# A graph attention, linear attention and mixture-of-experts layer: the waits of the first pass over the edges are given constants

## The reference

```python
xn = layernorm(x)                                   # x: 3125 nodes x 256
x = x + gnn(xn, edges) + mix(xn)                    # 53125 edges, sorted by dst, own edges included
x = x + ffn(layernorm(x))

def gnn(x, src, dst):                               # 4 heads of 64
    h = x @ W
    logits = leaky_relu(a_src(h)[src] + a_dst(h)[dst], 0.2)
    alpha = exp(logits - segment_max) / segment_sum(exp(...))
    return relu(segment_sum(alpha * h[src]) + bias)

def mix(x):                                         # 4 heads of 32
    q, k, v = x @ W_qkv; context = softmax(k over nodes)^T v
    return (q @ context) @ W_out + b_out

def ffn(x):                                         # 8 experts, 2 for each node, weighted
    return sum over the chosen e of w_e * (gelu(x @ W1[e] + b1[e]) @ W2[e] + b2[e])
```

## Time and profile before

| | us |
|---|---|
| three runs | 1038.55, 1036.66, 1035.8 |
| median | 1036.66 |
| span of the profiled execution | 1154.8 |
| the profiled execution's own time | none is recorded beside its span |

### The profile page before, as it was taken

The page is one execution under the profiler, slowest core; times in us unless marked ns, Lnnn a source line. Parts: engine busy times, 40 slices in busy tenths (PEclk is TensorE's granted clock), DMA queues, the critical chain, the costliest instruction groups (busy, mean ns, idle before and its releaser), DMA issues. The chain is left out here.

```text
span 1154.8 us, 18630 instructions
## 1 busy us (share of the span) xinstructions
PE 937.2 (81%) x5127; PEld 831.2 (72%) x5128; DVE 492.8 (43%) x1359; ACT 397.2 (34%) x1099; POOL 558.7 (48%) x572
## 2 busy tenths in 40 slices
PE   7949688676876678697577476699999999999995
PEld 6848577565666567576466364699999999999994
DVE  6664465565656456456457367511111111111110
ACT  4526242224324233233233222443333333333331
POOL 2254666666666666566656620523333333333331
PEclk8976867777678677667758676799999999999998
DMA  7333444444444434444434424865666555656561
GB/s 215 101 106 91 113 117 114 114 134 127 115 115 128 136 105 133 119 122 138 129 109 108 129 66 142 290 202 180 180 180 182 168 170 172 180 179 179 180 182 19
DMA packets 76492, 163.65 MB, mean 142 GB/s; under 512 B 11536, under 2 KB 40868, under 8 KB 76306
## 3 DMA queue, kind: packets, MB, share of 16 engines
q0 software_dynamic: 30144, 69.30, 24.6%
q1 hardware_dynamic: 45729, 93.15, 24.4%
q10 hardware_dynamic: 560, 0.52, 0.2%
HBM read 145.95 MB, written 16.99 MB: 141 GB/s over the span
## 5 line engine op out<-in xcount | busy, mean ns | idle before, releaser
L571 POOL DMA_INDIRECT gathered<-h_table,src_row x416 | 402.2, 967 | 227.1 <-issue 121.5
L890 PE MATMUL bank<-gathered,one_hot 128*128 128x260 f32 x832 | 289.8, 503 | 57.7 <-issue 39.0
L890 PEld LDWEIGHTS bank<-gathered,one_hot 128*128 128x128 f32 x832 | 202.9, 253 | 111.5 <-issue 73.7
L1714 ACT ACTIVATE hiddenT<-bank,b_slot 128x128 f32<-128x128 f32 x424 | 121.1, 369 | 248.7 <-PE bank L1747 248.7
L1692 POOL DMA_INDIRECT out<-y,add_index x53 | 84.4, 1593 | 246.3 <-DVE y L1805 122.9
L1747 PEld LDWEIGHTS bank<-xgT,acc 128*128 128x128 f32 x1696 | 200.0, 194 | 3.5 <-ACT xgT L1706 0.9
L1747 PE MATMUL bank<-xgT,acc 128*128 128x128 f32 x1696 | 200.4, 277 | 0.5 <-ACT xgT L1706 0.5
L834 PEld LDWEIGHTS bank<-adc,w_sb 128*128 128x128 f32 x832 | 141.6, 234 | 78.4 <-issue 67.9
L1769 PE MATMUL bank<-w_sb,hiddenT 128*128 x848 | 193.5, 381 | 0.0
L834 PE MATMUL bank<-adc,w_sb 128*128 x832 | 126.1, 269 | 74.0 <-issue 73.8
L1769 PEld LDWEIGHTS bank<-w_sb,hiddenT 128*128 128x128 f32 x848 | 157.0, 190 | 22.0 <-issue 1.9
(11 more groups left out here) (240 smaller groups left out, 670.9 us busy)
## 6 DMA issues: line engine op xcount, KB each, us to landing
acc<-in_L_ffn_W SPq DMA_DIRECT2D x53, 1024.0 KB
w_sb<-key_table SPq DMA_DIRECT2D x52, 256.0 KB
w_sb<-in_L_ffn_W SPq DMA_DIRECT2D x8, 1024.0 KB, 11.1
gathered<-h_table,src_row POOLq DMA_INDIRECT x416
h_table<-acc SPq DMA_DIRECT2D x25, 130.0 KB, 2.0
out<-w_sb SPq DMA_DIRECT2D x5, 512.0 KB
xn_table<-w_sb SPq DMA_DIRECT2D x5, 512.0 KB
xs<-in_x SPq DMA_DIRECT2D x3, 640.0 KB, 10.5
```

The lines of the kernel that those rows point to most:

```text
L571: pool.indirect_dma_start(gathered[:, r, j, :], None, h_table, bass.IndirectOffsetOnAxis(ap=src_row[:, t:t + 1], axis=0)).then_inc(gather_ ...
L890: mm = pe.matmul(sum_bank[r % SUMS][:, 0:ROW], one_hot[:, r, j, :], gathered[:, r, j, :], start=(j == 0), stop=(j == G - 1))
L1714: op = act.activation(hiddenT[:, k, g * P:(g + 1) * P], bank[1 + 2 * k + half][:, f * P:(f + 1) * P], ACT.Gelu, bias=b1_slot[:, k, g:g + 1])
```

## The change

The body of each engine's loop becomes a function `one_pass(c)`. The loop stays, and holds an If: where the pass counter isn't zero, the body is emitted as before with the register c; its Else holds the body emitted with c = 0, a Python integer, so that every count in it is a constant. The separate increments of `waited` inside the pass stay in the first and go from the second. DVE's two inner Ifs go: what they held stands in the plain body alone. The instructions of the pass are in the program twice, the general body first.

```diff
+            def every_pass(eng, passes, one_pass):
+                with eng.Fori(0, passes) as c:
+                    with eng.If(c != 0):
+                        one_pass(c)
+                    with eng.Else():
+                        one_pass(0)
+
+            def counted_wait(eng, c):
+                if not isinstance(c, int):
+                    eng.sem_inc(waited, 1)
...
                         sp.wait_ge(x_step, c * len(PIECES) + k + 1 + (k >= INSIDE))
-                        sp.sem_inc(waited, 1)
+                        counted_wait(sp, c)
...
-                    with sp.Fori(0, passes) as c:
+                    def one_pass(c):
                         sp.wait_ge(keys_ready, c + 1)
-                        sp.sem_inc(waited, 1)
+                        counted_wait(sp, c)
...
+                    every_pass(sp, passes, one_pass)
...
-                    with pool.Fori(0, passes) as c:
+                    def one_pass(c):
                         for s in range(NGRP):
                             r = s % RING

                             pool.wait_ge(summed, c * NGRP + s + 1)
-                            pool.sem_inc(waited, 1)
+                            counted_wait(pool, c)
...
+                    every_pass(pool, passes, one_pass)
...
                         act.wait_ge(hotT_ready, n + AHEAD)
-                        act.sem_inc(waited, 1)
+                        counted_wait(act, c)
...
-                    with pe.Fori(0, passes) as c:
+                    def one_pass(c):
                         pe.wait_ge(windows_ready, c * 2 + 2)
-                        pe.sem_inc(waited, 1)
+                        counted_wait(pe, c)
...
                         pe.wait_ge(hot_ready, c * NGRP + 5)
                         pe.wait_ge(ctx_taken, 1)
-                        pe.sem_inc(waited, 1)
+                        counted_wait(pe, c)
...
                         dve.wait_ge(stats2_ready, c * NT + PIECES[k][1])
-                        dve.sem_inc(waited, 1)
+                        counted_wait(dve, c)
...
-                    with dve.Fori(0, passes) as c:
+                    def one_pass(c):
...
-                        with dve.If(c == 0):
+                        if isinstance(c, int):
                             dve.wait_ge(kmax_spread, 1)
...
-                        with dve.If(c == 0):
+                        if isinstance(c, int):
                             dve.wait_ge(self_exp, 2)
```

More of the change, by code:

```diff
@@ L710, in step @@
                                     normalise_again(c, k, part)
-                    with act.Fori(0, passes) as c:
+                    def one_pass(c):
                         for r in range(FAR_ON):
@@ L733, in _ @@
                         turned_last(3, xnT2_last, bank[6][:, :])
+                    every_pass(act, passes, one_pass)
                 @block.tensor
@@ L928, in _ @@
                         mm.then_inc(gated, 1)
+                    every_pass(pe, passes, one_pass)
                 @block.vector
@@ L1371, in _ @@
                         add_bias(BATCHES[INSIDE][0], NT, bank[3][:, 0:(NT - BATCHES[INSIDE][0]) * NX].rearrange("p (t e) -> p t e", e=NX))
+                    every_pass(dve, passes, one_pass)
         b1_cols = sb(whole, "b1_cols", [P, NX * KF])
```

## The result

The changed kernel takes 1044.82 us (median of 7 runs, 1039.6 to 1046.62) against 1037.34 for the kernel before in the same rounds (7 runs, 1035.8 to 1039.34). The ratio is 1.0063, interval [1.0042, 1.0085]: 6.5 us slower. The prediction was no change, 1036.6 us, with a range up to 1041.

A forecast was written before the change was run, and what follows sets the result against it. POOL issuing gathers without a break, about 1.21 us each, was taken to bound the edge pass. Terms -0.5 - 0.5 - 1.0 + 1.9 gave about 0 on the median, 1036.6 us; range 1021 to 1041, likeliest case 1033.5 to 1039.8.

The forecast's parts named there:

- the fifth: Ifs on each engine: DVE's two go, each engine gets one with a long jump over the general body, +1.9 us.
- Who pays: At the pass's entry, only PE pays for the jump; idle time covers POOL, DVE and ACT: +1.9 us.
- The price: Jump over the general body: 2.1 us load latency plus 0.8 us per packet, 2.9 us for a waiting engine.
- PE's cover: Between context matmuls and first spread, PE's queued instructions hide 1 us of its jump.
- Step 1: Register arithmetic ahead of waits, all engines: about 1500 instructions go, hidden behind POOL's gathers, 0 us on the path.
- Step 2: POOL's wait moves onto a group's first gather: 0.53 us saved per really late wait, only one such, -0.5 us.
- Steps 2 and 3 together: POOL's wait on its gather -0.5 us; shorter hops before the first waiting gather -0.5, after the last -1.
- Step 4: SP's DMAs: none added or moved past another, SP not late for the pass, 0 us.
- the jump is paid more than once: Slower rival: PE's entry without cover and the pass's end, 2.9 us each, +4.8 us, 1041.5 us; chance 0.18.

The follow-up runs named there:

- base_again: The kernel before, unchanged, profiled a second time: span 1040.7 us, the execution itself 1043.38 us.
- base_third: The kernel before, unchanged, profiled a third time: span 1035.3 us, the execution itself 1037.2 us.
- pe_jump: The kernel before with PE's body of the pass twice, both on the register, so PE alone jumps: 1043.32 us, ratio 1.0032.
- dve_pe_register: The changed kernel with DVE and PE back on the register's loop; POOL, ACT and SP still jump: 1039.09 us, ratio 1.0011.
- pool_register: The changed kernel with POOL alone back on the register's loop; the other four engines jump: 1046.25 us, ratio 1.0070.
- act_sp_jump: The change on ACT and SP alone; POOL, PE and DVE keep the register's loop of the kernel before: 1037.69 us, ratio 0.9993.

## Why the prediction was wrong

The step that failed is the fifth, "Who pays". It had a price of 2.9 us for the jump, one payer, PE, and 1 us of cover: +1.9 us on the path. The runs showed two payers in series, DVE (3.4 us, and 1.5 of slower matmuls behind it) and PE (3.3 us). They put the first spread 8.2 us later; what reaches gather 32 is 5.7 to 6.7 us, and the time grew by 6.5. Its parts:

- **The price** was 0.2 to 1.7 us too low. Measured: 3.3 to 3.6 us on POOL, DVE and ACT, 3.4 to 4.6 on PE over four profiles, 3.1 at the pass's end. A taken branch as such is cheap: the fourth stage's loop branches back on PE in 0.08 to 0.25 us. By the rule of the Trainium skill (Runtime: NRT & Kernel Launch, Instruction fetch mechanics), a taken branch outside the pages held waits for a fetch; the trace agrees that the far one stalls, with these 3.1 to 4.6 us, but that it waits for a fetch no view shows. The instruction queue says little: 26 packets against the 24 of the earlier trace rows and of `base_again`, and 25 in `base_third`. No kernel varied the length of the body.
- **PE's cover** was right: its branch starts 1.0 to 1.1 us before the context's last matmul ends (80.9 against 81.98; 74.7 against 75.79 in pe_jump). But from the branch's start to the first spread 4.1 to 5.2 us pass, the branch's record and 0.6 to 0.9 us behind it, where the sum had 2.9. So PE stands still for 3.0 to 4.2 us in every kernel in which it jumps at the entry, and pe_jump alone costs 3.3 us.
- **DVE** was let off for 12.10 us of idle time before 100.93. That idle time lies behind the entry: DVE's pass begins with the shift of the keys, from which ACT makes the exponents and PE the context. In that work no wait is left to take up a delay, so DVE's 3.6 us (65.38 against 61.79 in `base_again`) reach the context as 3.44 and stand in series with PE's own jump. This second payer is the main miss.
- **POOL** was let off for 7.87 us of idle time before 89.38. That wait was of the disturbed execution. In two undisturbed ones POOL does not wait at all before gather 32, and the first sum is ready 1.4 to 2.3 us before POOL is. So POOL's jump is on the path when nothing else is (dve_pe_register), and is covered when the sum is later still (pool_register).
- **The clock** was in no step. It costs where PE waits longer for DVE's keys: the changed kernel's 50 context matmuls, behind idle stretches of 2.54 and 1.82 us, run at a granted clock of 0.79 and take 1.47 us more than those of `base_third`, at 1.00 (2.4 GHz) behind 1.07 us. Behind PE's own stop the spreading runs at 0.50 (1.2 GHz); the first row is the changed kernel, the three others `base_third`, the columns as in the earlier trace rows for PE alone:

```profile
85.20:92.10 6.90, 6.90 (x33) 0.50 0.63 161
```
```profile
75.90:78.80 2.90, 2.87 (x25) 1.00 0.72 179
80.40:82.20 1.80, 1.76 (x9) 0.50 0.56 181
82.90:86.50 3.60, 3.59 (x9) 0.51 0.59 179
```

  The kernel before falls to 0.50 as well, behind its 1.68 us wait before the last eight. From the first spread to the first sum's end it takes 10.6 and 10.7 us in its two profiles, and the kernels in which PE jumps at the entry 10.3 to 11.0. So here the lower clock adds little; it takes what the stop should have given back, since the wait of 1.68 us is gone behind it.

The other steps hold in the main. **Step 1:** 838 instructions went, not 1500, and neither the gathers' pitch nor, within the 2 us between two profiles, their total moved; that the register arithmetic hid fits this and isn't shown apart from the constants' gain. **Step 2:** a gather that is really late starts 0.28 and 0.27 us after the sum with a constant, 0.79, 0.79 and 0.80 with a register (pe_jump, act_sp_jump, pool_register): 0.5 us, and only one such wait of more than 0.6 us in the pass. **Steps 2 and 3 together** were put at 2.0 us less, and constants alone give 1.7 to 2.6, though no view shows where. **Step 4:** SP's jump at 47.8 showed nowhere by itself: the keys are stored at 64.23 in act_sp_jump and at 64.27 in `base_again`. It was not tried apart from ACT's.

Of the rivals, "the jump is paid more than once" had the sign and nearly the size (+4.8), but the wrong second place: the entry of DVE, not the pass's end, whose jump the order of the two bodies spares.

What stays open: the chain's 5.7 to 6.7 us less the constants' 2 us would be 4 to 5, and two comparisons gave 6.5. Their intervals reach down to 4.4, but 2 us may be missing in this account. The profiles can't place them: from gather 32 to the last one's end the unchanged kernel takes 485.5 us in one and 487.5 in the other.

## What to carry to other kernels

A branch taken over a long body cost each engine 3 to 5 us once here (one length of body was tried), so look at each engine's first instruction behind it and follow what it feeds: jumps of engines that feed each other add up, those side by side count once, and those of engines with nothing to do are free. Where the common case has to be one of two bodies, put the jump at the end at which the engines wait anyway. Take slack and "idle before" from an execution whose span agrees with the timed runs; where it doesn't, as with 1154.8 against 1036.66 us here, profile the same kernel again before costing anything by its waits.

## What the runs showed of the hardware

A far jump stalls PE inside the branch's own record (3.37 to 4.61 us, where the fourth stage's loop branch takes 0.08 to 0.25), but on POOL, DVE and ACT the record is over after 0.07 us at most and the stall is only the gap before the next instruction, labelled "issue". PE's granted clock fell behind stops of 3.0 to 4.2 us, and in the kernel before behind one of 1.68 us, to 0.50 (1.2 GHz) both times; the context's 50 matmuls took 7.44 to 8.94 us behind the longer waits that DVE's jump left, and 6.04 without. And one execution in three of an unchanged kernel showed 114 to 120 us more than the others (1154.8 against 1040.7 and 1035.3), in waits that no semaphore explained, without a difference in its code.
